# Two attention and expert layers on one core: tokens sorted by expert through DRAM, folded attention weights, one block ordered by a table

## The reference, cut to what matters

```python
x = x + L0_attn(L0_cond(x, mask, cond))     # 16 heads of 8, RMS norm, modulation by cond; then
                                            # rotary attention, 16 heads of 64 (32 of them rotated), causal
x = x + L0_ffn(L0_cond2(x))                 # quaternion rotation; 8 experts, 128 -> 512 -> 128, relu, top 2
x = x + L1_attn(L1_cond(x, cond))           # 8 experts, 128 -> 256 -> 256 -> 128, relu, top 2 of the softmax;
                                            # then attention with 8 heads of 128, decay and level weights, layer norm
x = x + L1_ffn(L1_cond2(x, mask, cond))     # the 16-head block again; then int8/ternary rounded
                                            # 128 -> 512, convolution of 3 taps, silu, 512 -> 128
# experts of layer 0, as the reference has them:
for e in range(NUM_EXPERTS):
    expert_mask = jnp.any(top_idx == e, axis=-1)
    h = jax.nn.relu(flat_x @ W1[e] + b1[e])
    y = h @ W2[e] + b2[e]
    w = router_weights[:, e] * expert_mask.astype(x.dtype)
    final_output = final_output + y * w[:, None]
```

## Time and profile before

| | before |
|---|---|
| median of 3 runs | 718.7 us |
| runs | 713.22, 718.7, 851.63 us |
| profiled execution, span | 711.2 us |
| instructions | 10053 |
| PE busy | 558.2 us, 78% of the span |
| DVE busy | 461.7 us, 65% |
| ACT busy | 295.9 us, 42% |
| POOL busy | 186.7 us, 26% |
| mean granted clock of PE | 0.914 of full speed |
| moved by DMA | 25.56 MB |

### The profile page before, as it was taken

The page is one execution under the profiler, slowest core; times in us unless marked ns, Lnnn a source line. Parts: engine busy times, 40 slices in busy tenths (PEclk is TensorE's granted clock), DMA queues, the critical chain, the costliest instruction groups (busy, mean ns, idle before and its releaser), DMA issues. The chain is left out here.

```text
span 711.2 us, 10053 instructions
## 1 busy us (share of the span) xinstructions
PE 558.2 (78%) x3794; PEld 397.6 (56%) x3794; DVE 461.7 (65%) x1036; ACT 295.9 (42%) x631; POOL 186.7 (26%) x147
## 2 busy tenths in 40 slices
PE   2374686569999978979879999999999678778542
PEld 2152575546665845736644767766676557656421
DVE  1369985955756487494851434667777978988663
ACT  0133354134444334444444343343555465646441
POOL 1546724610501161240301000130303043133210
PEclk9997988769999999999998999999999999999655
DMA  9200000000222211111213222112110000000000
GB/s 302 94 1 1 1 2 0 1 0 1 61 60 60 61 31 30 31 30 31 60 31 118 63 73 56 49 30 61 31 31 5 1 5 5 0 5 5 5 4 4
DMA packets 32895, 25.56 MB, mean 36 GB/s; under 512 B 6448, under 2 KB 29360, under 8 KB 32592
## 3 DMA queue, kind: packets, MB, share of 16 engines
q1 hardware_dynamic: 32368, 24.62, 11.7%
q10 hardware_dynamic: 480, 0.32, 0.2%
HBM read 24.40 MB, written 0.52 MB: 35 GB/s over the span
## 5 line engine op out<-in xcount | busy, mean ns | idle before, releaser
L450 ACT ACTIVATE hid<-PS,expert_b 128x512 f32<-128x512 f32 x128 | 87.5, 687 | 120.2 <-PE PS L418 86.9
L418 PE MATMUL PS<-featT,expert_w 128*128 128x512 f32 x192 | 98.9, 627 | 4.9 <-DVE xres L495 2.3
L434 PEld LDWEIGHTS PS<-expert_w,hid 128*128 128x128 f32 x768 | 88.7, 192 | 15.5 <-ACT hid L450 9.8
L434 PE MATMUL PS<-expert_w,hid 128*128 128x128 f32 x768 | 91.5, 276 | 0.9 <-ACT hid L450 0.9
L638 POOL TENSOR_TENSOR cond_kbd<-cond_qkv,const 128x2048 f32<-128x2048 f32 x16 | 59.9, 3741 | 63.4 <-ACT cond_qkv L723 63.3
L863 POOL TENSOR_TENSOR rot_sh<-rot_sh,const 128x1024 f32<-128x1024 f32 x16 | 52.4, 3295 | 38.4 <-DVE rot_sh L1036 38.4
L425 PE MATMUL PS<-hid,expert_w 128*128 128x512 f32 x128 | 60.8, 601 | 0.2
L418 PEld LDWEIGHTS PS<-featT,expert_w 128*128 128x128 f32 x192 | 32.0, 195 | 44.2 <-ACT hid L450 21.5
L495 DVE SCALAR_TENSOR_TENSOR xres<-PS,gatew,xres 128x128 f32<-128x128 f32 x64 | 18.0, 343 | 59.3 <-PE PS L434 59.3
L650 POOL TENSOR_SCALAR cond_st<-cond_st 128x1 f32<-128x1 f32 x16 | 5.8, 364 | 173.9 <-ACT cond_zn L738 173.7
L785 DVE STREAM_TRANSPOSE cond_ptbd<-cond_sm 32x512 f32<-32x512 f32 x64 | 45.0, 703 | 1.2
(11 more groups left out here) (221 smaller groups left out, 1092.7 us busy)
## 6 DMA issues: line engine op xcount, KB each, us to landing
expert_w<-in_moe_w_dram SPq DMA_DIRECT2D x48, 256.0 KB, 2.9
expert_w<-in_moe_w_dram SPq DMA_DIRECT2D x32, 128.0 KB, 2.5
wqk<-in_attn_qk_dram SPq DMA_DIRECT2D x2, 1024.0 KB, 6.2
wv<-in_attn_v_dram SPq DMA_DIRECT2D x2, 512.0 KB, 7.2
wout<-in_attn_out_dram SPq DMA_DIRECT2D x2, 512.0 KB, 8.4
last_b<-in_moe_last_b_dram SPq DMA_DIRECT2D x2, 512.0 KB, 6.1
xres<-in_x_dram SPq DMA_DIRECT2D x1, 512.0 KB, 5.2
cond_w<-in_cond_w_dram SPq DMA_DIRECT2D x2, 256.0 KB, 5.7
```

The lines of the kernel that those rows point to most:

```text
L418: mm = nc.tensor.matmul(full(at), w[:, P * f:P * f + P], featT[:, BANK * half:BANK * half + BANK], start=True, stop=True)
L434: mm = nc.tensor.matmul(full(at, E * j, E * j + E), h[:, 2 * layer + c, P * j:P * j + P], w[:, lo:lo + E], start=(c == 0), stop=(c == nf - 1))
L450: nc.scalar.activation(hid[e % 2][:, c, :], full(at), ACT.Relu, bias=WBIAS[g % WB][:, c:c + 1]).then_inc(ring_read[number % 2], 1)
```

## The change

1. **Experts on chosen tokens only.** A job is one half in one layer; four jobs run in the order (half 0, layer 0), (1, 0), (0, 1), (1, 1). In each, DVE and PE rank the tokens by expert (`j_choose`, `j_rank`, `j_slot`), which gives each of the 1024 choices a slot in 15 units of 128, every unit of a single expert. POOL scatters the tokens' rows to DRAM with 8 indirect transfers, SP loads the units back, a unit goes through its expert's weights (fetched by the computed expert number), DVE copies the result to `slots`, SP stores it to DRAM, and POOL gathers it with 8 indirect transfers; DVE adds the two results of a token with its two gates. The last bias is one small product for each tile (`j_bias`). There are 4 weight buffers in the first job, 7 after.
2. **Compact condition block.** Queries and values are masked by group of 32 (`c_queries`, `c_vals`, POOL, 128x512), keys by head within the group (`c_keys`, DVE); scores are 16 matmuls of 128 columns behind one that writes the mask; one transpose over 128 partitions; no block-diagonal buffer.
3. **Folded rotary block.** Value and output weights are multiplied once (`fr_turn`, `fr_mm`); queries and keys are parted into a rotated and a plain half, so that the rotation is on 128x512, all of it on DVE. Scores are 32 matmuls with 32 rows, values 4 matmuls of 512 columns on the normed features, and gain and shift come after. The two quaternion rotations and the router become one product (`rotmix`).
4. **Folded level attention.** Query times key and value times output weights are multiplied once (`fl_turn`, `fl_mm`), keys and values are the inputs themselves; its decay is turned by one transpose.
5. **Silu** by tanh and one DVE operation.
6. **One block.** The meeting of all engines between the phases goes. `WHEN` gives each step of each engine a due time, and `in_time_order` sorts by it. The loads at the start are in another order (the first two tiles first); POOL clears `slots`, and SP writes the zeros to DRAM for the four jobs. Buffers of the rotary block's queries, keys and probabilities are single; the condition block and the feed-forward have two sets, the feed-forward on two banks.

The core of the diff; the new functions stand in it as they are:

```diff
+UNITS = 2 * HT * P // P + EXPERTS - 1
+GROUP = 4
+JOBS = ((0, 0), (1, 0), (0, 1), (1, 1))
+WB_FIRST, WB = 4, 7
+WHEN = {
...
+    ("PE", "r_q"): (245, 419, 683, 894, 1098, 1359, 1627, 1887),
...
+    ("POOL", "scatter"): (1446, 2259, 2813, 3297),
...
+}
+def in_time_order(engine, steps):
+    todo = [(WHEN[engine, name][n], n, step) for name, step, count in steps for n in range(count)]
+    for _, n, step in sorted(todo, key=lambda entry: entry[0]):
+        step(n)
...
-                    ins = nc.vector.scalar_tensor_tensor(out=target[:, n, :], in0=full(at, E * j, E * j + E), scalar=gatew[:, j, e:e + 1],
-                                                         in1=target[:, n, :], op0=ALU.mult, op1=ALU.add)
...
+                def load_weights(n):
+                    p, i = n // UNITS, n % UNITS
+                    layer, w = JOBS[p][1], W[W_OF[n]]
+                    sp.wait_ge(done["routing"], place("j_slot", p + 1))
+                    if W_BEFORE[n] is not None:
+                        sp.wait_ge(done["m_y"], W_BEFORE[n] + 1)
+                    e = sp.value_load(unit_e[p % 2][0:1, i:i + 1], min_val=0, max_val=EXPERTS - 1)
...
+                def load_slots(n):
+                    p, g = n // GROUPS, n % GROUPS
+                    lo, hi = GROUP * g, GROUP * g + group_units(g)
+                    sp.wait_ge(scattered[p % 2], 16 * 2 * HT * (p // 2 + 1))
+                    if p:
+                        sp.wait_ge(stored_group[g], 16 * p)
+                    sp.dma_start(slots[:, lo:hi, :], xs_d[p].rearrange("(u s) e -> s u e", s=P)[:, lo:hi, :]).then_inc(slots_loaded[g], 16)
...
+                def scatter(p):
+                    pool.wait_ge(done["routing"], place("j_slot", p + 1))
...
+                    for j, n in enumerate(tiles_of(p)):
+                        src = xres[:, n, :] if layer else xf[:, n, 0:E]
+                        for c in range(2):
+                            at = HT * c + j
+                            nc.gpsimd.indirect_dma_start(xs_d[p], bass.IndirectOffsetOnAxis(slot[p % 2][:, at:at + 1], 0), src, None).then_inc(scattered[p % 2], 16)
+                def gather(n):
+                    p, j = n // HT, n % HT
+                    for g in range(GROUPS):
+                        pool.wait_ge(stored_group[g], 16 * (p + 1))
+                    if p:
+                        pool.wait_ge(done["m_comb"], n - HT + 1)
+                    for c in range(2):
+                        at = HT * c + j
+                        nc.gpsimd.indirect_dma_start(yt[:, c, j, :], None, ys_d[p], bass.IndirectOffsetOnAxis(slot[p % 2][:, at:at + 1], 0)).then_inc(taken[j], 16)
...
+                def r_scores(n):
...
+                    for g in range(4):
+                        for src in (qkr, qkp):
+                            for j in range(4):
+                                r = slice(S * j, S * j + S)
+                                ins = mm(full(j, P * g, P * g + P), src[r, g, :], src[r, 4 + g, :], start=(src is qkr), stop=(src is qkp))
...
+                def r_y(n):
...
+                    for b in range(SEQ):
+                        r = slice(S * b, S * b + S)
+                        ins = mm(full(b), czn[n % CZ][r, :], rpt[r].rearrange("p h t -> p (h t)"), start=True, stop=True)
...
+                def r_out(n):
...
+                    for h in range(AH):
+                        ins = mm(full(5, 0, E), ryT[:, h, :], wvo[:, h, :], start=(h == 0), stop=(h == AH - 1))
...
+                    for c in range((4, 2)[JOBS[p][1]]):
+                        ins = mm(full(at, P * c, P * c + P), w[:, P * c:P * c + P], xsT[i // GROUP % 2][:, i % GROUP, :], start=True, stop=True)
...
+                    nc.vector.transpose(cpt[s][:].rearrange("p h t -> p (h t)"), csm[s][:].rearrange("p h t -> p (h t)")).then_inc(done["c_probs"], 1)
...
+                def m_comb(n):
...
+                    own.mark(stt(out=here, in0=yt[:, 0, j, :], scalar=wgt[p % 2][:, j, 0:1], in1=here, op0=ALU.mult, op1=ALU.add))
+                    own.wait()
+                    stt(out=here, in0=yt[:, 1, j, :], scalar=wgt[p % 2][:, j, 1:2], in1=here, op0=ALU.mult, op1=ALU.add).then_inc(done["m_comb"], 1)
...
+                    stt(out=ys[s][:], in0=ys[s][:], scalar=1.0, in1=y[s][:].rearrange("p f b t -> p (f b t)"), op0=ALU.add, op1=ALU.mult).then_inc(done["f_silu"], 1)
```

More of the change, by code:

```diff
@@ L44 @@
 HID = 512
+NF = HID // P
 ROUND = 1.5 * 2.0 ** 23
@@ L239, in _, with go @@
             @block.scalar
             def _(act):
+                def go(out, src, func=ACT.Copy, **more):
+                    return nc.scalar.activation(out, src, func, **more)
                 act.dma_start(cond[:], d["cond"]).then_inc(loaded["small"], 16)
@@ new lines, in z_in @@
+                def z_in(half):
+                    here = z[:, HT * half:HT * half + HT, :]
+                    dve.wait_ge(done["levels"], place("u_z", half + 1))
+                    own.mark(tt(here, full(RING_BANK["u_z", half], 0, HT * NSMALL).rearrange("p (n c) -> p n c", c=NSMALL),
+                                small_b.unsqueeze(1).to_broadcast([P, HT, NSMALL]), ALU.add))
+                    own.wait()
+                    stt(out=za[:], in0=here, scalar=-1.0, in1=here, op0=ALU.mult, op1=ALU.min).then_inc(done["levels"], 1)
```

2366 lines of the change are left out of this document (1309 added, 1057 removed), and 15 rows, old and new, of the table WHEN.

## The result

The changed kernel takes 624.6 us (four runs, 618.06 to 626.65) against 717.0 us of the kernel before in the same measurement: a ratio of 0.871, 95% interval 0.865 to 0.877. The ratio leaves out one execution of the kernel before, which took 851.63 us. It is faster. The forecast was 598 us, range 555 to 680.

A forecast was written before the change was run, and what follows sets the result against it. PE was taken to bound the middle, a chain over all engines, DVE fullest, the two ends. Terms 141 + 94 + 80 + 130 + 9 + 134 + 2 gave 590, with 7.5 added 598 us; range 555 to 680.

The forecast's parts named there:

- Removed expert work: Experts: 60 units at 129 us replace 251.2 us of PE, 122 us less; DVE's 81.6 us become 64.
- Attention by tile: DVE per tile: first attentions 24.3 to 14.9 us, later ones 22.1 to 18.2; operations expected at their minimum times.
- Steps 1 and 6: Kernel's two ends: start to the fourth tile's features, 141 us; tail after the last gates, set by DVE's share, 134 us.
- step 3: Second half's first job through DRAM: routing, scatters, 15 units, store, gathers, combining 73 us, plus hand-overs, 80 us.
- Step 4: From second half's first job to its second: two jobs' units, gates, routing, later attentions; 130 us.
- The last 7.5 us: Whole kernel: added to the 590 us sum, since the runs' median 718.7 lay 7.5 above the profiled span.
- The clock: PE's granted clock falls with its load: 0.99 at 92% busy, 0.84 in the first stretch, 0.50 in the last.
- Rival B: Ends and hand-overs: waits shrink with the work, ends keep only DVE's bound, hand-overs cost 0; 567 us, chance 0.14.
- Rival C: POOL's indirect transfers: scatters and gathers cost 3.7 us each, +80, 678 us; chance 0.14.
- Rival D: POOL's indirect transfers: DVE holds off descriptor writing, 4.6 us each, +109, 707 us, or 736 at 5.5; chance 0.09.
- Rival E: Expert units: weights bound the jobs, 3.5 us a unit against 2.15, +61, 659 us; chance 0.05.
- A: Whole kernel: the main forecast as summed, 598 us, own range 570 to 630; chance 0.58.

The follow-up runs named there:

- chip 2: The changed kernel again, no edit, one execution on one of three chips; no waits put down to "remote"; 588.3 us.
- chip 1: The changed kernel again, no edit, four executions on another chip, with "remote" waits at all eight trains; 617.1 us.
- chip 15: The changed kernel again, no edit, on a third chip, with signals held at all eight trains; 623.0 us, ratio 0.869.
- the weights' bytes: Changed kernel with nearly all bytes of the weight loads left out, same issues and waits; 626.9 us against 617.1 unaltered.
- pairs: Changed kernel with keys' masked copy on ACT, plus POOL waiting for each pair of scatters or gathers to land; 629.8 us against 608.8 with whole trains.

## Why the prediction was right, and where it was off

The verdict, faster, came with the range holding the time. By the steps, with the changed kernel where signals are held and where not (each step from the ends of the same instructions):

| step | forecast | chip 2 | chip 1 | chip 15 | result's execution |
|---|---|---|---|---|---|
| 1 fourth tile's features | 141 | 138.3 | 135.5 | 135.9 | 135.8 |
| 2 four more tiles | 94 | 87.1 | 87.3 | 93.0 | 93.1 |
| 3 second half's first job | 80 | 93.3 | 111.9 | 113.2 | 114.9 |
| 4 to its second job | 130 | 126.1 | 138.9 | 140.8 | 139.6 |
| 5 gates | 9 | 10.7 | 9.6 | 10.7 | 10.4 |
| 6 tail | 134 | 129.0 | 127.2 | 129.0 | 129.0 |
| 7 store | 2 | 2.0 | 2.0 | 2.0 | 2.0 |
| span | 590 | 586.5 | 612.4 | 624.6 | 624.8 |

- **Removed expert work.** Right. PE's whole work was forecast at 442; it is 448.2 on chip 2 and 461.5 in the result's execution, where the clock is lower (0.839 against 0.864). DVE 350 forecast, 338.2 found. What the smaller expert work and the shorter attentions each gave of the 92 us was not run apart; the small transposes put back cost 63.5, and the experts' products doubled cost 70.7.
- **Attention by tile.** The transpose over 128 partitions was priced at 0.70 and takes 0.711, so the lower bound held. The minima did not hold in the mean: L1472 and L1433 take 0.87 and 0.91 us instead of 0.69 (0.69 in the median, 1.41 and 1.58 at most), and POOL's masks 1.41 and 1.22 instead of 1.14. The prediction had the stretching go away with POOL's long operations; it did not. Steps 1 and 6 came 3 to 7 us shorter all the same.
- **The route through DRAM, step 3.** The step that failed. Issuing was right: 0.96 to 1.08 us a transfer and 0.30 behind it, 1.26 to 1.38 against 1.2. On chip 2 the term of 80 measures 93.3: routing 6.3 (forecast 5.5), scatters 10.7 (9.6), landing and load to the first product 11.2 (7.4), 15 units 39.7 (37), the last store held in SP's queue 7.8 (nothing), its landing 4.8 (4.5, the store with its hand-over), gathers 9.8 (9.6) and the end 3.0 (5.7, landing and combining). The 13 us too little are the store's place in the queue (7.8) and the scatters' landing and load (3.8); a transfer lands in 3.5 to 4.6 us in the median there, where 1.5 to 2.9 were taken from the earlier trace rows. In the result's execution the step is 21.6 us longer still: 16.6 of these lie between the units' first product and last copy (56.3 us), where two trains run beside them, 6.0 ahead of the first product and 5.0 at the end, while the last store is held 2.6 us there and not 7.8.
- **Step 4** is 9 to 11 over the forecast where signals are held and 4 under it where not. It has three of the eight trains, step 3 has four.
- **The last 7.5 us** were not earned: the span of 711.2 belonged to one of the quicker executions of before, and a run of after is only 1.8 over its span. With 1.8 in their place the forecast is 592, 3.5 over chip 2 and 33 under the result. The closeness on chip 2 is in part luck: step 3 came 13 us over its term, and the steps 1, 2, 4 and 6 together 19 under theirs.
- **The clock.** The prediction has it fall with PE's load. The earlier trace rows has a row against that, 1.00 in the first 13.9 us at 12% busy, and so has the page of after, 1.00 at 44% in its first 13.9 us and 0.93 after it at 81%. No term of the sum rests on it.
- **Rival B** was half right at the ends (136 and 129 in the result's execution, B wanted 130 and 126) and fell in step 3: the hand-overs cost more, not nothing. **Rival C** is further off than the forecast (678 against 624.6), and its mechanism, 3.7 us an issue, is not there: the median issue is 0.96. **Rival D** shows once a train of scatters: a scatter takes 1.87 to 1.95 us where DVE's 128x480 multiplication (L1585, 1.03 us, two SBUF inputs) runs beside it, 1.32 in the first train; that is 0.4 to 1.0 us four times, not 3.4 on each of 32. **Rival E** fell with the weights' bytes. None of the rivals was a signal that comes late. That the result lies within the range, and even within A's own 570 to 630, is luck: no term of either stands for what took it from 588 to 625.

What was right for the right reason is the removed work of PE and DVE. What was not foreseen is the 29 to 36 us that lie between chip 2 and the others. No row of before could show them, since it has no indirect transfer. That they go with the held signals is seen in three traces of the unaltered kernel with them and one without. That the late signals cost them is argued, not shown: the edit that took all these waits away and left the transfers in place (pairs) also made the trains longer, and the granted clock differs too.

## What to carry to other kernels

When a kernel gets its first indirect transfers, look at the idle time of the *other* engines at the place of each train, and run it on more than one chip before settling on a number: here the same program is 588 or 617 to 625 us while its predecessor is 715 to 717 everywhere. Bound such a new thing's price from what it does to its neighbours, not from its own duration alone. And in a sum, a transfer that follows a queue's other issues costs its place in the queue: ask which issues are ordered just ahead of the one that everybody waits for (moving the last store ahead of the nine weight loads was not tried).

## What the hardware showed that I had not expected

- Beside eight indirect transfers of POOL in a row, 0.30 us apart, signals of PE reach ACT and DVE up to 7 us late, with 79 to 95 us of idle time in all over the two engines (10.1 the longest), on two chips and in the result's execution; on a third chip, in one execution, the same trains held nothing. SP's six issues beside a train take 8.2 to 8.9 us there instead of 5.1. Plain transfers in the same queue (0.56 us each), or indirect ones of which at most two are unlanded, hold none.
- DVE and POOL still stretch each other by 0.2 to 0.3 us an operation of 128x512 (0.69 to 0.91, 1.07 to 1.39), though no multiplication of POOL is over 1.6 us long.
- PE's mean granted clock rose when the units' products were doubled, 0.846 to 0.887, and fell to 0.805 when DVE had more to do between them. In the result's execution it is 0.79 in the stretch where PE is busy 68% of the time and 0.93 from 13.9 to 135.8 us, at 81%.
- On chip 2 a 256 KB store to DRAM landed in 4.6 us in the median (3.7 in the result's execution), an indirect scatter of 64 KB in 3.9 to 4.2, a plain one in 3.0 to 3.2.
